# Last layer's pair stage: state products grouped, scores in 64-row halves, increments moved behind the next step's first projection

## The reference, cut to what matters

```
zxbca = x @ W_in.T                      # x, z, b, c per head (32 heads, 64 wide), and a
decay = exp(-exp(a))                    # one number per head and token
state = state * decay + x_t b_t^T       # 64 x 64 per head
y_t   = state c_t + x_t * D
y     = layernorm(y * silu(z)) @ W_out.T
```

## Time and profile before

| | |
|---|---|
| median of 3 runs | 4075.12 us (4071.56 to 4076.61) |
| profiled execution | 4091.38 us |
| its span, first to last instruction | 4089.6 us |
| TensorE busy over the span | 3655.6 us |
| VectorE busy | 2325.4 us |
| ScalarE busy | 1598.5 us |
| GpSimd busy | 1389.7 us |
| pair stages, first sequence | about 2891 to 3280 us |
| pair stages, second sequence | about 3365 to 3753 us |

### The profile page before, as it was taken

One profiled execution on the slowest core, in us unless ns is written; L12 is line 12 of the kernel. 1 busy time (PEld: TensorE's weight loads), 2 busy tenths in 40 slices (PEclk: granted clock), 3 DMA queues, 4 the chain that ended last, 5 costly groups with the idle time before them and its releaser, 6 DMA issues. The chain is left out here.

```text
span 4089.6 us, 65022 instructions
## 1 busy us (share of the span) xinstructions
PE 3655.6 (89%) x21096; PEld 2662.2 (65%) x21096; DVE 2325.4 (57%) x4783; ACT 1598.5 (39%) x2884; POOL 1389.7 (34%) x1087
## 2 busy tenths in 40 slices
PE   6999999999797999999966799997899979999676
PEld 4777777777575888888833344443678737776354
DVE  3555555555325566666647778774566646666444
ACT  2444444444233444444423166662333333333211
POOL 1333333333135666666614000000223352334254
PEclk8999999999898999999978799998899989999755
DMA  0000000000001000000004122210333313332144
GB/s 35 5 5 5 3 5 5 5 3 5 32 0 45 18 17 20 18 17 17 8 3 183 42 74 76 76 65 26 83 82 87 90 34 76 91 82 54 57 103 95
DMA packets 115990, 178.66 MB, mean 44 GB/s; under 512 B 22288, under 2 KB 65040, under 8 KB 115600
## 3 DMA queue, kind: packets, MB, share of 16 engines
q1 hardware_dynamic: 109776, 169.38, 13.8%
q0 software_dynamic: 6144, 8.39, 1.3%
HBM read 151.51 MB, written 25.95 MB: 43 GB/s over the span
## 5 line engine op out<-in xcount | busy, mean ns | idle before, releaser
L424 POOL TENSOR_TENSOR l0h_probs<-l0h_probs,l0h_inv 128x128 f32<-128x128 f32 (+7 forms) x256 | 292.8, 1146 | 585.7 <-DVE l0h_inv L459 585.7
L1747 DVE TENSOR_REDUCE l2h_half<-l2h_s 128x1 f32<-128x512 f32 x512 | 329.6, 685 | 94.2 <-PE l2h_s L1658 94.1
L1734 ACT ACTIVATE l2h_PT<-l2h_s 128x1024 f32<-128x1024 f32 x256 | 261.9, 1023 | 194.2 <-PE l2h_s L1668 194.2
L355 PE MATMUL l0h_sc<-l0a_KT,l0h_QT 128*128 x768 | 296.7, 499 | 30.0 <-ACT l0h_probs L528 28.3
L382 PE MATMUL l0h_cx<-l0h_PT,l0h_VG 128*128 128x128 f32 x2304 | 300.7, 276 | 0.0
L528 ACT ACTIVATE l0h_probs<-l0h_sc,l0h_negtop 128x128 f32<-128x128 f32 (+7 forms) x256 | 189.6, 741 | 245.4 <-DVE l0h_negtop L454 245.0
L382 PEld LDWEIGHTS l0h_cx<-l0h_PT,l0h_VG 128*128 128x128 f32 x2304 | 278.0, 192 | 1.1
L159 POOL TENSOR_TENSOR XN<-XN,n_rstd 128x512 f32<-128x512 f32 x32 | 39.8, 1265 | 635.2 <-DVE n_rstd L140 635.2
L2189 DVE TENSOR_TENSOR_SCAN l3p_table<-l3p_decb,l3p_eye 128x512 f32<-128x512 f32 x128 | 149.8, 1212 | 116.0 <-DMA l3p_prow<-l_decays 92.2
L1658 PE MATMUL l2h_s<-l2h_K,l2h_Q 128*128 128x512 f32 x512 | 180.2, 429 | 21.7 <-DMA l2h_K<-l_split 18.0
L452 DVE TENSOR_REDUCE l0h_top<-l0h_sc 128x1 f32<-128x128 f32 (+7 forms) x256 | 194.0, 758 | 8.8
(11 more groups left out here) (410 smaller groups left out, 9081.1 us busy)
## 6 DMA issues: line engine op xcount, KB each, us to landing
l3p_decb<-l_decays SPq DMA_DIRECT2D x128, 256.0 KB, 5.2
l3p_w<-L_w SPq DMA_DIRECT2D x34, 512.0 KB, 5.9
l2h_Q<-l_split SPq DMA_DIRECT2D x64, 256.0 KB
l2h_K<-l_split SPq DMA_DIRECT2D x64, 256.0 KB
l3p_prow<-l_decays SPq DMA_DIRECT2D x128, 128.0 KB, 5.6
l_split<-l2q_hi SPq DMA_DIRECT2D x16, 512.0 KB, 4.0
l_split<-l2q_lo SPq DMA_DIRECT2D x16, 512.0 KB, 3.8
mx_wgu<-L_ffn_w_gate_up SPq DMA_DIRECT2D x32, 256.0 KB
```

The costliest lines, as they stand in the source:

```text
L355: mm = pe.matmul(sc[u % 2][:, lo:lo + n], QT[:, u * P:(u + 1) * P], KT[:, ds(g, 1), b * S + lo:b * S + lo + n], start=True, stop=True)
L424: pool.tensor_tensor(p, p, inv[:, u % 4:u % 4 + 1].to_broadcast([P, keys(u)]), ALU.mult).then_inc(probs_scaled, 1)
L1734: act.activation(PT[:, b, kb, :], s2[kb % 2][:, :], ACT.Exp, scale=L2_SCALE).then_inc(exped, 1)
L1747: dve.reduce_max(half[:, b, t, z:z + 1], s1[i % 2][:, :], AX_X).then_inc(maxed, 1)
```

## The change: what it does

- In `outputs` the state products of all blocks come first, then the half-width products of all blocks.
- Scores are made with 64-row operands, one matmul per head and block, each head's into a bank of its own; `cT2` with its zeros becomes `cT`, copied in one instruction, and GpSimd's memset of it goes. mixT reads them without rearranging.
- TensorE's increments of step n are given to it in step n + 1, between the x projection and the other three.
- On VectorE the masking of the increments and the chain of states of step n (now `carry`) stand in step n + 1 between the first and the second table scan, and `add_skip` behind cdT.
- SyncE's list is unchanged.

The core of the diff:

```
 # TensorE, outputs
+carried = range(0 if z > 0 else 1, QUAD)
+for t in carried:
+    col = slice(t * P, (t + 1) * P)
+    pe.matmul(py[:, col], state[:, o, t, :], cdT[:, o, col], start=(t == carried[0]), stop=False, skip_group_check=True)
 for t in range(QUAD):
     col = slice(t * P, (t + 1) * P)
-    inter = t > 0 or z > 0
-    if inter:
-        pe.matmul(py[:, col], state[:, o, t, :], cdT[:, o, col], start=True, stop=False, skip_group_check=True)
     for i in range(2):
         half = slice(i * L3_HD, (i + 1) * L3_HD)
-        mm = pe.matmul(py[half, col], xtok[:, o, t, half], mixT[:, o, i, col], start=not inter, stop=True, ...)
+        mm = pe.matmul(py[half, col], xtok[:, o, t, half], mixT[:, o, i, col], start=False, stop=True, ...)

 # TensorE, scores
 for t in range(QUAD):
-    mm = pe.matmul(psc[:, 2 * t * P:2 * (t + 1) * P], bT[:, t * P:(t + 1) * P], cT2[:, :, t * P:(t + 1) * P], start=True, stop=True)
+    for i in range(2):
+        half = slice(i * L3_HD, (i + 1) * L3_HD)
+        mm = pe.matmul(psc[:, i * BANK + t * P:i * BANK + (t + 1) * P], bT[half, t * P:(t + 1) * P], cT[half, t * P:(t + 1) * P],
+                       start=True, stop=True)

 # TensorE, step
-    project(h, z)
+    project(h, z, (0,))
     if not is_first(h, z):
+        increments(*before(h, z))
+    project(h, z, (1, 2, 3))
+    if not is_first(h, z):
         outputs(*before(h, z))
-    tables_and_states(h, z)         # turns, scores, increments
+    turns_and_scores(h, z)

 # ScalarE
-act.activation(cT2[0:L3_HD, 0, :], pc[0:L3_HD, :], ACT.Copy)
-act.activation(cT2[L3_HD:P, 1, :], pc[L3_HD:P, :], ACT.Copy).then_inc(c_kept, 1)
+act.activation(cT[:, :], pc[:, :], ACT.Copy).then_inc(c_kept, 1)

 # VectorE, step
 dve.wait_ge(loaded_d[o], 64 * h + 64)
-for i in range(2):
-    dve.tensor_tensor_scan(table[:, i, :], ...)
-if not is_first(h, z):
-    add_skip(*before(h, z))
+dve.tensor_tensor_scan(table[:, 0, :], ...)
+if not is_first(h, z):
+    carry(*before(h, z))            # dsm, then the chain of states
+dve.tensor_tensor_scan(table[:, 1, :], ...)
 ...                                 # cdT
+if not is_first(h, z):
+    add_skip(*before(h, z))
 ...                                 # btok, mixT
-...                                 # dsm, the chain of states

 # behind the last step
+increments(L3_PAIRS - 1, NZ - 1)    # TensorE
+carry(L3_PAIRS - 1, NZ - 1)         # VectorE
```

More of the change, by code:

```diff
@@ L1978, in l3_pairs @@
         xT, bT = st.sb("xT", [P, 2, BANK]), st.sb("bT", [P, BANK])
-        cT2 = st.sb("cT2", [P, 2, BANK])
+        cT = st.sb("cT", [P, BANK])
         cdT = st.sb("cdT", [P, 2, BANK])
@@ L1990, in l3_pairs @@
         psc = st.ps("psc", 2 * BANK)
-        loaded_w4, loaded_c, loaded_d, consts, zeroed = st.sem("loaded_w4"), st.sem("loaded_c"), [st.sem(f"loaded_d{i}") for i in range(2)], st.sem("consts"), st.sem("zeroed")
+        loaded_w4, loaded_c, loaded_d, consts = st.sem("loaded_w4"), st.sem("loaded_c"), [st.sem(f"loaded_d{i}") for i in range(2)], st.sem("consts")
         x_made, b_made, c_made, z_made = st.sem("x_made"), st.sem("b_made"), st.sem("c_made"), st.sem("z_made")
@@ L2046, in _, with project @@
             def _(pe):
-                def project(h, z):
+                projections = ((px, x_made, xt_kept), (pb, b_made, bt_kept), (pc, c_made, c_decayed), (pz, z_made, z_kept))
+                def project(h, z, which):
                     n = NZ * h + z
@@ L2051, in project @@
                     tok = slice(z * BANK, (z + 1) * BANK)
-                    for i, (bank, made, used) in enumerate(((px, x_made, xt_kept), (pb, b_made, bt_kept), (pc, c_made, c_decayed), (pz, z_made, z_kept))):
+                    for i in which:
+                        bank, made, used = projections[i]
                         wait(pe, used, n)
@@ L2055, in project, with increments @@
                                       lambda c: XH[:, c, tok], lambda c: XL[:, c, tok]).then_inc(made, 1)
+                def increments(h, z):
+                    n, o = NZ * h + z, z
+                    pe.wait_ge(bt_kept, n + 1)
+                    pe.wait_ge(xt_kept, n + 1)
+                    wait(pe, ds_masked, n)
+                    for t in range(QUAD):
+                        mm = pe.matmul(pds[:, t * P:(t + 1) * P], btok[:, t, :], xtok[:, o, t, :], start=True, stop=True)
+                    mm.then_inc(ds_made, 1)
                 def outputs(h, z):
@@ L2062, in outputs, with turns_and_scores @@
                     wait(pe, skipped, n)
+                    carried = range(0 if z > 0 else 1, QUAD)
+                    for t in carried:
+                        col = slice(t * P, (t + 1) * P)
+                        pe.matmul(py[:, col], state[:, o, t, :], cdT[:, o, col], start=(t == carried[0]), stop=False, skip_group_check=True)
                     for t in range(QUAD):
                         col = slice(t * P, (t + 1) * P)
-                        inter = t > 0 or z > 0
-                        if inter:
-                            pe.matmul(py[:, col], state[:, o, t, :], cdT[:, o, col], start=True, stop=False, skip_group_check=True)
                         for i in range(2):
                             half = slice(i * L3_HD, (i + 1) * L3_HD)
-                            mm = pe.matmul(py[half, col], xtok[:, o, t, half], mixT[:, o, i, col], start=not inter, stop=True,
+                            mm = pe.matmul(py[half, col], xtok[:, o, t, half], mixT[:, o, i, col], start=False, stop=True,
                                            skip_group_check=True)
                     mm.then_inc(y_made, 1)
-                def tables_and_states(h, z):
+                def turns_and_scores(h, z):
                     n, o = NZ * h + z, z
@@ L2086, in tables_and_states @@
                     for t in range(QUAD):
-                        mm = pe.matmul(psc[:, 2 * t * P:2 * (t + 1) * P], bT[:, t * P:(t + 1) * P], cT2[:, :, t * P:(t + 1) * P], start=True, stop=True)
+                        for i in range(2):
+                            half = slice(i * L3_HD, (i + 1) * L3_HD)
+                            mm = pe.matmul(psc[:, i * BANK + t * P:i * BANK + (t + 1) * P], bT[half, t * P:(t + 1) * P], cT[half, t * P:(t + 1) * P],
+                                           start=True, stop=True)
                     mm.then_inc(sc_made, 1)
[L2089 to L2096, removed]
                 def step(h, z):
-                    project(h, z)
+                    project(h, z, (0,))
+                    if not is_first(h, z):
+                        increments(*before(h, z))
+                    project(h, z, (1, 2, 3))
                     if not is_first(h, z):
                         outputs(*before(h, z))
-                    tables_and_states(h, z)
+                    turns_and_scores(h, z)
                 steps(pe, step)
+                increments(L3_PAIRS - 1, NZ - 1)
                 outputs(L3_PAIRS - 1, NZ - 1)
@@ L2139, in _ @@
             def _(pool):
-                pool.memset(cT2[:, :, :], 0.0).then_inc(zeroed, 1)
                 pool.memset(ysum[:, :], 0.0).then_inc(summed, 1)
@@ L2181, in add_skip, with carry @@
                                              op0=ALU.mult, op1=ALU.add).then_inc(skipped, 1)
-                def step(h, z):
+                def carry(h, z):
                     n, o = NZ * h + z, z
-                    dve.wait_ge(loaded_d[o], 64 * h + 64)
-                    wait(dve, mixed, n)
-                    wait(dve, bt_kept, n)
-                    for i in range(2):
-                        dve.tensor_tensor_scan(table[:, i, :], decb[:, o, i, :], eye4[:, :], 0.0, ALU.mult, ALU.add).then_inc(tables, 1)
-                    if not is_first(h, z):
-                        add_skip(*before(h, z))
[L2192 to L2204, removed]
                     dve.wait_ge(ds_made, n + 1)
@@ L2220, in step @@
                         op.then_inc(states if t == (QUAD - 1 if z + 1 < NZ else QUAD - 2) else linked, 1)
+                def step(h, z):
+                    n, o = NZ * h + z, z
+                    dve.wait_ge(loaded_d[o], 64 * h + 64)
+                    wait(dve, mixed, n)
+                    wait(dve, bt_kept, n)
+                    dve.tensor_tensor_scan(table[:, 0, :], decb[:, o, 0, :], eye4[:, :], 0.0, ALU.mult, ALU.add).then_inc(tables, 1)
+                    if not is_first(h, z):
+                        carry(*before(h, z))
+                    dve.tensor_tensor_scan(table[:, 1, :], decb[:, o, 1, :], eye4[:, :], 0.0, ALU.mult, ALU.add).then_inc(tables, 1)
+                    dve.wait_ge(c_kept, n + 1)
+                    wait(dve, y_made, n - 1)
+                    dve.tensor_tensor(cdT[:, o, :], pc[:, :], prow[:, o, :], ALU.mult).then_inc(c_decayed, 1)
+                    if not is_first(h, z):
+                        add_skip(*before(h, z))
+                    dve.wait_ge(tables, 2 * n + 2)
+                    dve.wait_ge(bt_made, n + 1)
```

(8 more changed lines are left out.)

## The result

The changed kernel takes 4228.92 us (median of 4 runs, 4225.94 to 4230.71) against 4075.86 for the kernel before: ratio 1.0377, 95% interval 1.0359 to 1.0395, or 153 us more. The forecast was 94 us more, with 4195 as the upper end of the range. Direction and place were right, the size was not.

What follows compares the result with a forecast made beforehand. The prediction took TensorE as the bound, busy 385.9 of 389.0 us. Loop +29 us, savings outside it -7 and clock +72 made +94 us on the median, 4169 us; range 4092 to 4195.

Steps and rivals of the forecast that it cites:

- Outputs 2.00 and 1.77 us: TensorE's outputs in the two steps of a pair, grouped: 2.00 and 1.77 us instead of 3.05 and 2.73.
- Scores 1.1 us, the row halves side by side: TensorE's scores as 16 passes in 64-row halves, run in pairs: 1.1 us instead of 1.72.
- rival B: TensorE's row halves run one after another, scores 2.1 us: 4127 us without slow stretches, 4199 with; chance 6%.
- The even step's carry queued behind the scan that waits; loop from the skip: On VectorE the carry stands behind the scan waiting for decays, delaying TensorE's odd-step outputs: 24.9 us a pair against 23.93.
- Skip to scan: From the end of VectorE's add_skip to the start of the odd step's scan, by way of SyncE's loads: 8.2 us.
- Even steps did not stall: TensorE's even-step outputs would not wait: scan and carry end at 5.9 us, outputs are due at 6.6.
- The loop's own +22 us: Whole kernel with the clock unchanged: +29 us over 30 pairs, -7 us outside the loop.
- Carry 2.1 us: VectorE's mask, copy and three state updates, in the loop ahead of TensorE's odd-step outputs: 2.1 us.
- The clock, 2.4 us a pair: TensorE at half clock behind its wait in all 30 pairs: 2.4 us lost each (1.9 to 2.9), 72 us together.
- The wait itself: TensorE's idle ahead of the odd step's state products, once a pair: 3.7 us as the profile counts.
- The range: Time of the changed kernel: 4154 to 4184 us as the forecast's own range, 4092 to 4195 as the wider one.

Runs made afterwards that it cites:

- e2: The changed kernel with VectorE's carry ahead of the first scan and its wait for the decays: 4043.35 us, ratio 0.9911 to the kernel before.
- e3: The changed kernel with dcol kept once for each half, so the odd step's decays no longer wait for add_skip: 4001.85 us, ratio 0.9811 to before.
- both together: The changed kernel with w_lo made after the even step's states and five unused products in TensorE's wait: 4114.12 us, ratio 1.0092 to before.
- e1: The changed kernel with GpSimd making the next weights' remainder w_lo only after the even step's states: 4156.45 us, ratio 1.0199 to before.
- e4: The changed kernel with five unused f32 products on TensorE ahead of the odd steps' wait for the states: 4174.4 us, ratio 1.0241 to before.

## Why the prediction was wrong, point by point

- *Outputs 2.00 and 1.77 us.* Right: 0.99 + 1.03 and 0.76 + 1.02 at full clock, start to next start.
- *Scores 1.1 us, the row halves side by side.* Right: 1.09 (rival B was wrong). The change into row halves also costs 0.09 us in the transposes ahead, which the sum did not have.
- *The even step's carry queued behind the scan that waits; loop from the skip.* Right in place: 30 waits of the scan, 30 of TensorE, and either cut of the loop ends the loss (e2, e3). Skip to scan was 8.06 us on the mean of 30, for 8.2. Even steps did not stall: 10.64 us, for 8.6 + 2.0. The loop's own +22 us came out at about 22 (the estimate under both together).
- *Carry 2.1 us.* **This is the step that failed.** It took 4.2 us in all 30 pairs, since one update took 2.3 to 2.5 us beside w_lo. I took its length from the place that it was leaving, and wrote of the weights' splitting only that it keeps its place and TensorE would not wait for it. In the new place w_lo falls on the updates in every pair. By the timeline both hang on loads that SyncE issues one behind the other after the same skip, prow at 3012.52 and the weights at 3014.33; that this is why they meet was read, not tested. 30 x 2.1 = 63 us; taking it away gave 72, the rest of it through the clock (e1). The forecast's 4169 and 63 make 4232; measured 4229.
- *The clock, 2.4 us a pair.* The mechanism was right and the size near: in the changed kernel state products and column halves took 1.58 + 1.91 us behind the wait instead of 0.76 + 1.02, with transposes and scores up to 1.3 more, 2.2 a pair in all (66 us, for 72); e4 got back 1.8 a pair. The wait itself was 5.55 us on the mean, not 3.7, which is the same 2.1 once more, less what the loads gained.
- *The range.* Its upper end, 4195, covered the clock's bounds and nothing for the carry, the one term on the loop to which I gave no bounds. An entry of the trace before would have given them: over the state's tile, VectorE's updates had a maximum of 1127 ns at a median of 352:

```profile
L2218 DVE SCALAR_TENSOR_TENSOR l3p_state<-l3p_state,l3p_prow,l3p_dsm x192: 350/352/1127, 2904.3 to 3747.8; 128x128 f32<-128x128 f32 x192
```

25 of the 192 lay beside one of GpSimd's operations of 1.3 us. The 17 long ones are all among them, and each ends 0.15 us behind that operation; the other eight began in its last 0.2 us and took 0.35, as did all the rest. Behind GpSimd's 2.34 us the bound would have been some 352 + 2340 = 2.7 us, an estimate from these rows.

## What to carry to other kernels

Work that an engine does ahead of a wait is not the same work behind it: whatever moves past a wait of its in-order engine inherits that wait, and then a wait that was free in the trace before can set the period of the loop. Trace who asks for the awaited load; here the one buffer of a 0.5 KB column set the pace, and a second buffer for it was worth more (0.9811) than the carry ahead of the scan (0.9911). When an instruction moves in time, look up the spread of its duration, not its median, and what the other engines do in the new place.

## What the runs showed of the hardware

In these traces an operation of VectorE with two operands in SBUF and an elementwise operation of GpSimd did not get on side by side. Beside w_lo the update took 2.3 to 2.5 us instead of 0.35 and ended 0.15 us behind it (in each of the 30 pairs of the changed kernel; the two records start within 0.34 us, in 17 pairs the update's first by up to 0.05). With a scan under way for 0.25 us it was w_lo that took 3.12 us instead of 2.34 (e1, 30 pairs). Skip, cdT and btok, which have one operand in PSUM, kept their 0.75, 0.68 and 0.68 us beside w_lo, and mixT its 1.22 beside GpSimd's sum of 1.3 us (the kernel before). The Trainium skill, GPSIMD Engine Reference, section Specifications, says that GpSimd's SBUF interfaces are shared with VectorE, with contention where a VectorE instruction has two SBUF inputs; the traces agree.

Pairs of 64-row matmuls ran side by side like the 64-column ones: 16 passes of 128 columns in 1.09 us to the next product's start, against 8 of 256 in 1.72, with 0.09 us more in the transposes ahead and, where increments follow, 0.1 more in these.

Behind waits of 5.0 to 6.3 us TensorE's clock was low in each of the 30 pairs of the changed kernel (granted clock 0.50 from 3024.0 to 3027.5 us), and ten passes without use in the wait kept it at 1.00 in 28 of 30. In between the length of the wait alone does not tell: in e1 the clock was whole behind 3.1 to 3.4 us in five pairs, and low behind 3.05 us in another.
